# Eight-batch cross-attention and mixture-of-experts kernel: the query weights' magnitude in a group of its own, shared scales in the drain, shared weights' splits a step sooner

## The reference

```python
x = x + xattn(layernorm(x), ctx, Wq, Wkv, Wout)   # 16 heads of 32, causal mask over 64 keys
# xattn: q = xn @ Wq.T; k, v = split(ctx @ Wkv.T); softmax(mask(q k^T / sqrt(32))) v @ Wout.T
x = x + ffn(layernorm(x), ...)
# ffn:  logits = xn @ router.T; the top 2 of 8 experts, weighted by their raw logits
#       expert: (silu(xn @ wg) * (xn @ wu)) @ wd;  inner width 256
#       plus a shared expert with biases: (silu(xn@sg_w+sg_b) * (xn@su_w+su_b)) @ sd_w + sd_b
```

## Time and profile before

| | before |
|---|---|
| median of 3 runs | 799.03 us (797.09 to 800.49) |
| the profiled execution | 799.31 us |
| its span (first to last instruction) | 797.2 us |
| PE busy | 763.4 us (96%) |
| DVE, ACT, POOL busy | 580.3 us (73%), 460.7 us (58%), 435.0 us (55%) |

### The profile page before, as it was taken

One profiled execution on the slowest core, in us unless ns is written; L12 is line 12 of the kernel. 1 busy time (PEld: TensorE's weight loads), 2 busy tenths in 40 slices (PEclk: granted clock), 3 DMA queues, 4 the chain that ended last, 5 costly groups with the idle time before them and its releaser, 6 DMA issues.

```text
span 797.2 us, 21959 instructions
## 1 busy us (share of the span) xinstructions
PE 763.4 (96%) x7249; PEld 523.3 (66%) x7249; DVE 580.3 (73%) x1194; ACT 460.7 (58%) x847; POOL 435.0 (55%) x563
## 2 busy tenths in 40 slices
PE   4998999999999999989999999999999999999995
PEld 2767878888888888768888874455555555454552
DVE  5899989999999898745798775565555555555552
ACT  4786889989888989765556333333333333333330
POOL 3454687777777777534210203656556565656543
PEclk9999999999999999999999999999999999999998
DMA  8426668787776767867756655989899888889892
GB/s 290 124 81 178 198 184 225 203 234 211 206 204 203 212 201 215 226 159 235 271 169 213 219 167 115 162 139 152 151 142 160 151 148 149 144 133 158 146 147 35
DMA packets 138318, 140.73 MB, mean 177 GB/s; under 512 B 87872, under 2 KB 88896, under 8 KB 137856
## 3 DMA queue, kind: packets, MB, share of 16 engines
q1 hardware_dynamic: 122336, 104.01, 48.0%
q0 software_dynamic: 15904, 35.70, 26.0%
HBM read 71.61 MB, written 52.31 MB: 155 GB/s over the span
## 4 chain that ended last, share of the span: by engine, by line
PE 78%; DVE 7%; DMA 6%; issue 3%; ACT 3%; POOL 2%; SPq 0%; POOLq 0%; DVEq 0%; ACTq 0%
PE psum L1431 43%; PE psum L1495 18%; PE psum L1422 9%; PE psum L1545 4%; DMA out<-w_q,tabs 3%; PE psum L1588 2%; DMA hidT<-xn2p 2%; DVE kv_store L966 1%; DVE head_max L1142 1%; DMA exp_all<-wvT 1%; DMA x_in<-normed_tokens,tabs 1%; DVE stats L1057 1%; PE psum L1474 1%; DVE probsT L966 0%; POOL w_sh L600 0%
## 5 line engine op out<-in xcount | busy, mean ns | idle before, releaser
L726 POOL DMA_INDIRECT out<-w_q,tabs x71 | 112.5, 1584 | 110.3 <-DVE w_q L1411 74.8
L716 POOL DMA_INDIRECT x_in<-normed_tokens,tabs x71 | 71.0, 999 | 89.9 <-DVE tabs L1292 42.2
L917 ACT ACTIVATE silu_g<-psum,tabs 128x256 f32<-128x256 f32 x71 | 33.6, 473 | 146.5 <-PE psum L1431 146.5
L1396 DVE SCALAR_TENSOR_TENSOR hid<-psum,tabs,silu_g 128x256 f32<-128x256 f32 x71 | 34.4, 484 | 111.7 <-ACT silu_g L917 111.7
L1431 PE MATMUL psum<-exp_all,hidT 128*128 x426 | 103.4, 379 | 3.0 <-DMA hidT<-xn2p 3.0
L1431 PE MATMUL psum<-exp_all,probsT 128*128 x420 | 96.4, 379 | 0.0
L1495 PE MATMUL psum<-xn1T,w_q 128*128 128x128 f16 x1536 | 91.0, 219 | 0.8 <-DVE maxima L949 0.8
L1431 PE MATMUL psum<-w_o,attnT 128*128 128x512 f16 x384 | 88.0, 379 | 0.8 <-DVE w_o L966 0.4
L1495 PEld LDWEIGHTS psum<-xn1T,w_q 128*128 128x128 f16 x1536 | 86.3, 98 | 2.1 <-issue 2.0
L572 POOL TENSOR_TENSOR exp_all<-piece,exp_all 128x512 f32 (+1 forms) x48 | 56.2, 1170 | 46.5 <-ACT piece L746 46.5
L1431 PEld LDWEIGHTS psum<-exp_all,hidT 128*128 128x128 f16 x426 | 41.7, 98 | 53.9 <-issue 5.6
(11 more groups left out here) (216 smaller groups left out, 1648.8 us busy)
## 6 DMA issues: line engine op xcount, KB each, us to landing
x_in<-x SPq DMA_DIRECT2D x64, 256.0 KB, 3.0
exp_all<-experts SPq DMA_DIRECT2D x24, 512.0 KB, 5.1
out<-xy SPq DMA_DIRECT2D x32, 256.0 KB, 3.1
normed_tokens<-xn SPq DMA_DIRECT2D x32, 256.0 KB, 5.0
normed_turned<-xn2T SPq DMA_DIRECT2D x32, 256.0 KB, 3.5
w_q<-out SPq DMA_DIRECT2D x32, 256.0 KB, 2.9
out<-w_q SPq DMA_DIRECT2D x32, 256.0 KB, 2.2
probsT<-normed_turned SPq DMA_DIRECT2D x16, 256.0 KB, 4.1
```

What stands on the lines that cost most here:

```text
L716: pool.indirect_dma_start(x_in[:, t % 4, :], None, xn_dram, bass.IndirectOffsetOnAxis(gather_at[:, t:t + 1], 0)).then_inc(gathered[t % 4], 16)
L726: pool.indirect_dma_start(out, bass.IndirectOffsetOnAxis(add_at[:, t:t + 1], 0), y[:, t % Y_RING, :], None, bounds_check=TOKENS - 1, oob_i ...
L917: act.activation(silu_g[:, :], psum[:, GU_BANK[m % 2], 0:I], ACT.Silu, scale=gate_scale_at[:, tm:tm + 1]).then_inc(silu_ready, 1)
L1396: dve.scalar_tensor_tensor(hid[:, :], psum[:, GU_BANK[m % 2], I:2 * I], up_scale_at[:, tm:tm + 1], silu_g[:, :], ALU.mult, ALU.mult).then_ ...
```

## The change

It makes group 1 of w_q's magnitude alone and runs it ahead of the context's, which become group 2 (the old groups 2 and 3 are now 3 and 4). On PE the four key products are no longer broken by a turn and a spread; on ACT w_q's high half comes ahead of the sums over the output weights, and the first values' high half moves behind tile 1's `xn1`; on DVE w_q's first low half comes ahead of group 2's reduction and its second behind it, and the context's scales are made in step 1 in `context_scales`. The shared expert's scales that only its own products use (ten operations) move from steps 6 and 7 into step 32, `shared_scales`, with a semaphore `shared_scaled` that the first entry waits for. The shared pieces are copied in steps 6, 7 and 8 on ACT, two each; POOL makes their low halves in steps 7 to 10 (two, two, one, one), now behind `xn2p`'s low half.

```diff
-SHARED_PIECES = ((0, 1), (2, 3, 4), (5,))
+SHARED_HIGHS = {6: (0, 1), 7: (2, 3), 8: (4, 5)}
+SHARED_LOWS = {7: (0, 1), 8: (2, 3), 9: (4,), 10: (5,)}
-M_CTX, M_WK, M_WV, M_WQ, M_WO, M_R, M_GU, M_DOWN, M_BIAS = range(9)
+M_WQ, M_CTX, M_WK, M_WV, M_WO, M_R, M_GU, M_DOWN, M_BIAS = range(9)
-GROUPS = ((M_CTX, M_WO), (M_WO, M_GU), (M_GU, N_MAG))
+GROUPS = ((M_WQ, M_CTX), (M_CTX, M_WO), (M_WO, M_GU), (M_GU, N_MAG))
-MAG_BANK = (6, 4, 5)
+MAG_BANK = (5, 4, 4, 5)
...
@@ POOL, step
                     pool.tensor_tensor(xn2p[:, 1, :], xn2[:, (j + 1) % 2, 0:H], xn2p[:, 0, :],
                                        ALU.subtract).then_inc(xn2_parts, 1)
+                if isinstance(tile, int) and tile in SHARED_LOWS:
+                    shared_lows(tile)
...
@@ ACT, first_weights
+                act.wait_ge(wq_scale_ready, 1)
+                for half in range(2):
+                    here = slice(half * C * H // 2, (half + 1) * C * H // 2)
+                    copy(w_q[:, 0, here], wq_raw[:, here], sc[:, S_TMP:S_TMP + 1], wq_hi)
                 act.wait_ge(wo_in, 32)
                 row_sums(M_WO, wo_raw)
                 act.wait_ge(sums_ready, 1)
                 row_sums(M_R, r_raw)
-                act.wait_ge(wq_scale_ready, 1)
-                for half in range(2):
-                    here = slice(half * C * H // 2, (half + 1) * C * H // 2)
-                    copy(w_q[:, 0, here], wq_raw[:, here], sc[:, S_TMP:S_TMP + 1], wq_hi)
                 act.wait_ge(k_mm, 1)
                 act.wait_ge(scales_ready, 1)
                 copy(k_all[:, 0, :, :].rearrange("p c k -> p (c k)"), bank(0, 4), sc[:, S_K:S_K + 1], k_hi)
-                high_values(0)
...
@@ ACT, entry
                     if tm is None:
+                        if m == 0:
+                            act.wait_ge(shared_scaled, 1)
...
@@ DVE, first_weights
                 turn_first(0)
+                largest(1)
+                spread_maxima(1)
+                powers(1)
+                dve.tensor_scalar(col(sc, S_TMP), col(inv2, M_WQ), W_UP, None, ALU.mult).then_inc(wq_scale_ready, 1)
                 dve.wait_ge(ctx_in, 64)
                 magnitude(M_CTX, staged[0])
                 magnitude(M_WK, wk_sb)
                 magnitude(M_WV, wv_sb)
-                largest(1)
-                spread_maxima(1)
-                powers(1)
-                dve.tensor_scalar(col(sc, S_TMP), col(inv2, M_WQ), W_UP, None, ALU.mult).then_inc(wq_scale_ready, 1)
                 dve.wait_ge(wq_scale_ready, 1)
+                query_low(0)
+                largest(2)
+                query_low(1)
...
+            def context_scales():
+                spread_maxima(2)
+                powers(2)
                 link(dve.tensor_scalar(col(sc, S_K), col(inv2, M_WK), col(inv2, M_CTX), KV_UP, ALU.mult, ALU.mult))
...
@@ DVE, first_splits
-                for half in range(2):
-                    here = slice(half * C * H // 2, (half + 1) * C * H // 2)
-                    dve.wait_ge(wq_hi, half + 1)
-                    low(w_q[:, 1, here], wq_raw[:, here], col(sc, S_TMP), w_q[:, 0, here], wq_split)
-                largest(2)
+                context_scales()
+                largest(3)
                 dve.wait_ge(k_hi, 1)
...
@@ DVE, second_scales and shared_scales
-                powers(3)
+                powers(4)
+                dve.tensor_scalar(inv2[:, M_GU:N_MAG], inv2[:, M_GU:N_MAG], W_UP, None, ALU.mult).then_inc(scales_ready, 1)
+
+            def shared_scales():
+
                 link(dve.tensor_scalar(col(sc, S_GU), col(pow2, M_GU), XW, None, ALU.mult))
...
@@ DVE, step
-                if isinstance(b, int) and (b, j) == (1, 3):
-                    third_scales()
+                if isinstance(b, int) and (b, j) == (B, 0):
+                    shared_scales()
...
@@ PE, first_products
+                turn_magnitudes(1)
+                spread_magnitudes(1)
                 pe.wait_ge(ctx_in, 4 * 16)
                 for c in range(C):
-                    if c == 1:
-                        turn_magnitudes(1)
-                        spread_magnitudes(1)
                     last = pe.matmul(psum[:, c, :].rearrange("p (b k) -> p b k", b=B), wk_sb[:, c * P:(c + 1) * P],
                                      ctx_sb[:, :, 0, :], start=True, stop=True)
                 last.then_inc(k_mm, 1)
                 turn_magnitudes(2)
-                pe.wait_ge(scales_ready, 1)
+                pe.wait_ge(xn1T_ready, 1)
                 values(0)
+                spread_magnitudes(2)
+                turn_magnitudes(3)
```

69 lines of the change are left out of this document (38 added, 31 removed).

## The result

The changed kernel took **805.25 us** (median of 5 runs, 798.91 to 806.5) against 799.03 (797.09 to 800.49): ratio 1.0071, 95% interval 1.0043 to 1.0099. So it is slower, by more than half a per cent in the middle and by a little less at the low end. The two intervals don't touch.

A forecast was written before the change was run, and what follows sets the result against it. TensorE, busy 96%, was taken as the bound, behind one chain until 24.7 us and VectorE until 87. Terms 1.6 + 1.7 − 0.8 − 1.9 − 1.6 + 3.2 + 1.7 = +3.9 on 799.31 gave 803.2 us (798.5 to 807.5).

The forecast's parts named there:

- The keys' new wait: Start: later context scales on DVE delay ACT's keys and then the first values, +1.6 us, bounds +1.0 to +3.0.
- Half rate behind the gap: Start: PE's gap before tile 1 grows to 3.3 us and half rate follows, +1.7 us, bounds 0 to 4.15.
- Step 6: Fill: DVE loses five scale operations and gains a 128x3 one, −0.8 us, between gains of 0.45 and 1.35.
- step 7: Fill: the other scale operations leave and PE's clock stays at 2.4 GHz, −1.9 us, bound −0.2.
- POOL's backlog: Steps 9 to 11: fewer shared pieces on POOL, behind xn2p, remove PE's wait, −1.6 us, bounds −1.2 and −1.8.
- Ten operations in step 32: Drain: chained scale operations on DVE before head_max delay attn by their whole length, +3.2 us, between 2.2 and 3.8.
- Half rate in step 33: Drain: PE's gap before attn's transposes becomes 3.4 us and half rate follows, +1.7 us, bounds 0 to 1.7.
- 3 us or more: Sign of being right: the length of PE's gap in step 33, with a second half-rate stretch there.
- the drain has room: Rival, drain: attn is not what PE waits for, so −3.2 and −1.7 us, 798.3 us; chance 0.13.
- The clock holds at both gaps: Rival, start and step 33: no half rate follows either longer gap, 799.8 us; chance 0.15.
- The keys' new wait is worse: Rival, start: late clock in the keys (+1.4) and longer half rate behind the gap (+1.0), 805.6 us; chance 0.2.
- Faster: Rival: early w_q shortens the start by some 1.5 us and the drain hides its operations, 793.5 us; chance 0.07.

The follow-up runs named there:

- filler_start: Changed kernel plus 30 products that nothing reads on PE, in its gap before tile 1's transposes; 804.59 us, ratio 1.0077.
- start_only: Kernel before with only the new start (w_q's own group, new order of keys and context scales); 801.86 us, ratio 1.0041.
- scales_34: Changed kernel with the ten shared scale operations in step 34 instead of 32; 797.89 us, ratio 0.9999.
- drain_only: Kernel before with only the ten shared scale operations moved to step 32; 800.42 us, ratio 1.0026.
- split_only: Kernel before with the shared pieces a step sooner and the operation freeing their scales in step 6, ahead of the ten; 796.31 us, ratio 0.9979.
- filler_drain: Changed kernel plus 18 products that nothing reads on PE, behind the queries of step 33; 802.43 us, ratio 1.004.
- mended: scales_first with the context's group turned and spread between the key products and the ten operations in step 34; 795.86 us, ratio 0.9969.
- scales_first: Changed kernel with the context's scales ahead of w_q's second low half and tile 1's statistics, their spread ahead of the first values; 798.44 us, ratio 0.9998.
- after_again: Changed kernel measured once more, unaltered, in another group; 799.51 us, ratio 1.0009.

## Why the prediction was right or wrong

The forecast was 803.2 us (798.5 to 807.5), +3.9 on the profiled execution. Both medians, 805.25 and 799.51, lie in the range, which is 9 us wide; the first is 2 us above the forecast and the second 3.7 below it, and no term of the sum explains either. What bears the forecast out is the traces, +4.0 and +3.3 us at step 34, and the parts measured alone, which add up to +3.7. By the terms of its sum:

- **The keys' new wait, +1.6.** The mechanism is right, the size was short: tile 1 starts 2.37 us later (27.12 against 24.75). The step that failed is the clock within the keys. I carried the moment of the rise over from the one execution of before and let the keys end at 16.3; they ended at 17.41, all at 1.2 GHz. In profiles of other kernels with the same start, up to there, they took 5.19 to 6.71 us, so this varies from run to run. The queue behind the keys took 3.86 us where I had 4.15. Bounds of +1.0 to +3.0 held it.
- **Half rate behind the gap, +1.7.** The gap was 3.43 (3.3 said), the price 1.65, shown by filler_start. start_only and scales_34 had a longer stretch behind the same gap: from the transposes to the second queries 7.63 and 7.39 us instead of 4.81, which is +2.8 and +2.6, within the bound of 4.15.
- **Step 6, −0.8, and step 7, −1.9.** PE's gap shrank by 0.48. I had the choice between a held and an unheld 128x3 operation and took the middle; it was held, as its rows beside a POOL operation had shown before. The clock stayed at 2.4 GHz behind 1.51 us, worth 1.67. Together −2.2 from step 7 to 8, where −2.5 was forecast. drain_only shows that it is the scale operations that bring this.
- **POOL's backlog, −1.6.** The interval from step 8 to 12 lost 2.2, of which 0.22 had been put down to step 7; the remaining 2.0 is above my bound of 1.8. split_only shows the same 37.59, so it is the splits alone. I had counted the waits of PE and not the stretch around them.
- **Ten operations in step 32, +3.2.** `attn` came 2.07 us later (326.63, with 0.30 us of older delay, against 324.26). The failed step is the price: I carried over the two held operations of steps 6 and 7, and none was held here. The Trainium skill's "SBUF — State Buffer", section "Summary: rules for kernel authors", was read as saying that the operations with two SBUF inputs or two columns are held in the drain too; it says that the second to issue blocks until the first finishes. In step 6 it agrees: the 128x3 operation started 0.03 us behind POOL's and took as long, 1.16. In step 32 POOL's operation ran from 320.30 to 321.46. L1060, with two SBUF inputs, had started 0.10 us ahead of it and took 0.16; the 128x2 one started 0.19 us before its end, took 0.23 and ended 0.04 us behind it. Nothing there speaks against the rule; I had left out where POOL would stand. That left the ten at 2.07 us, near the 2.2 that I had given for none held.
- **Half rate in step 33, +1.7.** It was 1.63, and filler_drain takes 1.67 away. It came behind a gap of 2.09 us instead of 3.4 ("3 us or more" was one of the signs of being right, and it failed), so the reason that I gave, a gap longer than both earlier ones, was wrong; filler_start shows that it need not come.

Against the forecast the keys' wait is 0.8 us dearer and the ten operations 1.1 cheaper, step 6 gains 0.3 less and the backlog 0.4 more. The sum, +3.3 for the four intervals, is near +3.9 partly because these offset each other. The rival "the drain has room" falls: `attn` was what PE waited for. It is true two steps later, which scales_34 shows. "The clock holds at both gaps" falls too, in all five profiles that have the change's own start unfilled, and in four of the five with the ten operations in step 32 and no filler there. "The keys' new wait is worse" (805.6) is true in its first half: the keys ended at 17.41, near the late bound of 17.65. Its second half, the longer half rate, is in start_only and scales_34 and in neither trace of the changed kernel. That the first median of 805.25 lies so near its time is not shown to come from it, since the profile with the late keys is only 4.0 us behind at step 34. "Faster" needed DVE's queue not to hold `scales_ready`; mended comes nearest to that, and even there the second queries are 0.2 us later than before.

## What to carry to other kernels

Before work moves to an earlier place, look at what its queue stands before there: w_q's split was on no chain and still held up the keys, since DVE does both in order and the keys' scales wait for a turn on PE that had moved behind all key products. Small chained operations cost their whole length wherever the engine is just in time, and nothing two steps later where it waits for another; here the same ten operations cost 3.7 us in step 32 and none in step 34. A saving or a loss of half a microsecond before a TensorE gap can decide over 1.7 us of half rate behind it, so take gaps of the trace, not only busy time, as terms of the sum.

## What the runs showed of the hardware

- **Half rate behind a gap is not a matter of the gap's length alone.** In these traces the gaps of 1.07 and 1.5 us were not followed by it, nor one of 1.66 at 505 us in filler_start; those of 1.99, 2.57 and 3.43 were, and one of 2.11 at 508 us in filler_drain; a gap of 2.21 in scales_first and mended was not. The gap of 2.1 in step 33 was followed by it in four profiles and not in filler_start's. The one of 2.97 at 341 to 350 us, which all fourteen profiles have, was followed by it in nine, the kernel before and after_again among them, and not in five, the changed kernel's first among them. One such stretch cost 1.6 to 1.7 us; in start_only and scales_34 it cost 2.8 and 2.6.
- **TensorE's first rise to 2.4 GHz moves from run to run.** The eight halves of the keys, unbroken from 10.45 to 10.72 us on, took 6.75 and 6.64 us in the two profiles of the changed kernel, and 6.71, 6.30, 5.73, 5.45, 5.25 and 5.19 in six kernels that are the same up to there. The Trainium skill's "TensorE: Matmul & The Clock Gate", section "What's actually happening", calls the number of slow products at a kernel's start variable from run to run; these eight profiles agree.
- **Small VectorE operations are held only where they fall.** In step 6 the 128x3 operation started behind POOL's and ended 0.03 us behind it, after 1.16 us. The 128x2 one ended 0.02 us behind POOL's in step 34 (0.42 us long) and 0.04 us behind it in step 32 (0.23 us). Four 128x1 ones that started beside the same POOL operation in step 32 took 0.15 to 0.21 each.
- **Executions of one kernel differ by up to 10.7 us** in a group, and two measurements of the same kernel by 0.6%, with intervals that exclude each other. Here a verdict at half a per cent took two groups and a ledger from the traces.
